# A graph network on one core: ranks by source placed in two halves of 392 columns, and rows normalised four blocks a turn

## The reference

```python
edge_index = jnp.stack([src, dst])
h = jnp.maximum(_layernorm(x, axis=-1), 0.0)
x = x + _L0_gnn_ref(h, src, dst, edge_weight, L0_gnn_weight, L0_gnn_b)
h = jnp.maximum(_layernorm(x, axis=-1), 0.0)
x = x + _L1_gnn_ref(h, edge_index, edge_attr_128, node_vec1, node_vec1_n2, ...)
h = jnp.maximum(_layernorm(x, axis=-1), 0.0)
x = x + _L2_gnn_ref(h, edge_index, edge_weight, ...)
h = jnp.maximum(_layernorm(x, axis=-1), 0.0)
x = x + _L3_gnn_ref(h, L3_gnn_relvectors, ..., src, dst, edge_type_16)
return x
```

## Time and profile before

| what | before |
|---|---|
| median of 3 timed runs | 5067.49 us (5064.09 to 5072.64) |
| span of the profiled execution | 6606.6 us |
| time of the profiled execution outside its span | not given |
| DVE, busy share of the span | 56% |
| POOL, busy share of the span | 54% |
| TensorE (PE), busy share of the span | 57% |
| preparation in the trace | 0 to 1492.6 us |
| scatters of records, L462 | 784, 808.2 us busy |

### The profile page before, as it was taken

How to read it: one execution, slowest core, us unless ns; L and a number is a source line. 1 busy time by engine, 2 the same in 40 slices (tenths; PEclk the granted TensorE clock), 3 DMA queues, 4 the chain that set the end, 5 groups by cost and what they waited for, 6 DMA issues and landing times. The chain is left out here.

```text
span 6606.6 us, 98591 instructions
## 1 busy us (share of the span) xinstructions
PE 3748.5 (57%) x15612; PEld 2748.4 (42%) x15613; DVE 3700.6 (56%) x12722; ACT 1475.8 (22%) x5078; POOL 3595.2 (54%) x4000
## 2 busy tenths in 40 slices
PE   0000020005776776776677777777779667777676
PEld 0000010004555554555455555555559534444443
DVE  5249691006666666666555555555557656555555
ACT  1000000000111111111455455555546301100000
POOL 4640686755655565555444444444437766655554
PEclk9999999998887888888788888878889878888888
DMA  4320224454444444444333333333332233333332
GB/s 119 85 68 0 73 83 89 118 148 120 127 127 123 125 128 124 127 128 111 93 94 94 96 95 95 94 93 94 97 95 86 89 88 94 91 91 90 90 90 72
DMA packets 505174, 651.54 MB, mean 99 GB/s; under 512 B 86113, under 2 KB 381294, under 8 KB 504944
## 3 DMA queue, kind: packets, MB, share of 16 engines
q0 software_dynamic: 150160, 395.04, 20.9%
q1 hardware_dynamic: 354913, 255.45, 14.3%
HBM read 550.09 MB, written 100.06 MB: 98 GB/s over the span
## 5 line engine op out<-in xcount | busy, mean ns | idle before, releaser
L1398 POOL DMA_INDIRECT a_row<-h_rows,a_idx x832 | 789.8, 949 | 944.0 <-PE a_p_s L1504 396.0
L2005 POOL DMA_INDIRECT r_row<-h_rows,r_idx x832 | 798.3, 960 | 528.7 <-PE r_p_s L2046 267.9
L462 POOL DMA_INDIRECT src_records<-rec,pos_slot x784 | 808.2, 1031 | 419.6 <-issue 250.3
L983 POOL DMA_INDIRECT s_row<-h_rows,s_rec x832 | 804.5, 967 | 281.0 <-issue 242.2
L1018 PE MATMUL s_sums<-s_row,s_hotw 128*128 128x256 f32 x1664 | 661.3, 484 | 519.5 <-DVE s_hotw L1203 315.3
L2046 PE MATMUL r_p_s<-r_row,r_hot 128*128 128x272 f32 x1664 | 644.8, 502 | 362.8 <-DVE r_row L2182 171.9
L1481 PE MATMUL a_p_q<-nodes,a_hotT 128*128 x1664 | 665.0, 486 | 314.9 <-DVE a_score L1551 188.9
L1211 DVE TENSOR_TENSOR nodes<-nodes,s_sums 128x385 f32 x832 | 455.5, 548 | 509.1 <-remote 290.8
L1504 PE MATMUL a_p_s<-a_row,a_masked 128*128 128x257 f32 x1664 | 588.7, 439 | 178.1 <-issue 124.3
L2046 PEld LDWEIGHTS r_p_s<-r_row,r_hot 128*128 128x128 f32 x1664 | 353.1, 234 | 678.8 <-issue 296.2
L1551 DVE CUSTOM_DVE_ANT_0 a_prod<-a_p_q,a_row 128x258 f32<-128x258 f32 x832 | 352.7, 424 | 415.9 <-DMA s_rec<-src_records 187.6
(11 more groups left out here) (315 smaller groups left out, 7511.6 us busy)
## 6 DMA issues: line engine op xcount, KB each, us to landing
s_rec<-src_records SPq DMA_DIRECT2D x832, 66.0 KB
a_locs<-dloc_rows SPq DMA_DIRECT2D x208, 256.0 KB
rec<-in_edge_attr SPq DMA_DIRECT2D x98, 448.0 KB
s_row<-h_rows,s_rec POOLq DMA_INDIRECT x832
a_row<-h_rows,a_idx POOLq DMA_INDIRECT x832
r_row<-h_rows,r_idx POOLq DMA_INDIRECT x832
src_records<-rec,pos_slot POOLq DMA_INDIRECT x784
x_rows<-X SPq DMA_DIRECT2D x1, 6272.0 KB
```

The source lines that it names most:

```text
L462: gp.indirect_dma_start(out=src_records, out_offset=bass.IndirectOffsetOnAxis(ap=pos_slot[:, k:k + 1], axis=0), in_=rec[:, k, :], in_offse ...
L983: gp.indirect_dma_start(out=row[:, k % R, :], out_offset=None, in_=env["h0_rows"], in_offset=bass.IndirectOffsetOnAxis(ap=rec[:, k % R, DS ...
L1398: gp.indirect_dma_start(out=row[:, k, 0:D], out_offset=None, in_=env["h2_rows"], in_offset=bass.IndirectOffsetOnAxis(ap=idx[:, k:k + 1], a ...
L2005: gp.indirect_dma_start(out=row[:, k % R, 0:D], out_offset=None, in_=env["h3_rows"], in_offset=bass.IndirectOffsetOnAxis(ap=idx[:, k:k + 1 ...
```

## The change

The ranks are placed in two halves of 392 columns, written out one after the other, in place of eight segments of 98 in a loop. The place writes to `pos["src"]` directly, and `pos_seg` with its two copies goes. The second half has no carry. The helper unrolls three blocks a turn (`RB`) in place of six. `ranked_steps` rises twice, by 392. POOL's power and its wait move from before turn 16 to before turn 22 (`ROOT_TURN`). ScalarE's wait for `rstd_ready` moves from before turn 16 to before turn 28 (`FIRST_FOUR`), and it normalises four blocks in each of the turns 28 to 39.

```diff
-    SEG = STEPS // 8
+    SEG = STEPS // 2
...
-    PAIRS = (BLOCKS - 1) // 2
-    FIRST_PAIR = 16
+    RB = 3
+    AT_ONCE = 4
+    FOURS = (BLOCKS - 1) // AT_ONCE
+    ROOT_TURN, FIRST_FOUR = 22, 28
...
-        eq = sb(ctx, "eq", [EP, SB, SEG], U16)
-        cum_seg = sb(ctx, "cum_seg", [EP, SB, SEG])
+        eq = sb(ctx, "eq", [EP, RB, SEG], U16)
+        cum_seg = sb(ctx, "cum_seg", [EP, RB, SEG])
...
-                scatters((0, FIRST_PAIR))
+                scatters((0, ROOT_TURN))
                 gp.wait_ge(stats_ready, 1)
                 nc.gpsimd.tensor_tensor(rstd[:], vare[:], half[:], ALU.pow).then_inc(rstd_ready, 1)
-                scatters((FIRST_PAIR, WIN_TURN))
+                scatters((ROOT_TURN, WIN_TURN))
...
-                with ac.Fori(0, FIRST_PAIR) as turn:
+                with ac.Fori(0, FIRST_FOUR) as turn:
                     complete(turn)
                 ac.wait_ge(rstd_ready, 2)
                 ac.wait_ge(loaded_x, 32)
-                with ac.Fori(0, PAIRS) as pair_i:
-                    complete(pair_i + FIRST_PAIR)
-                    normalise(pair_i * 2)
-                    normalise(pair_i * 2 + 1)
+                with ac.Fori(0, FOURS) as four:
+                    complete(four + FIRST_FOUR)
+                    for k in range(AT_ONCE):
+                        normalise(four * AT_ONCE + k)
...
+                def place_half(seg):
+                    cols = slice(seg * SEG, (seg + 1) * SEG)
+                    n = seg * BLOCKS
...
+                        nc.vector.copy_predicated(pos["src"][:, cols], eq[:, k, :], cum_seg[:, k, :]).then_inc(placed, 1)
...
+                    if seg == 0:
+                        in_turns(ve, BLOCKS, RB, (2, place), (2, carry), (1, count_up), (0, match))
+                        own_wait(ve, carried, n + BLOCKS)
+                    else:
+                        in_turns(ve, BLOCKS, RB, (2, place), (1, count_up), (0, match))
+                    own_wait(ve, placed, n + (BLOCKS + 1))
+                    ve.nop().then_inc(ranked_steps, SEG)
```

More of the change, by code:

```diff
@@ L250, in prepare @@
     HOT_TURNS = STEPS // 16
+    assert FOURS * AT_ONCE == BLOCKS - 1 and ROOT_TURN < FIRST_FOUR and FIRST_FOUR + FOURS < STORE_TURN
     assert HOT_TURNS * 16 == STEPS and SEGS * SEG == STEPS and WIN_TURN + (CHUNKS - 1) * WIN_APART < REC_TURNS
@@ L263, in prepare @@
         lo_d = sb(ctx, "lo_d", [EP, STEPS], BF16)
-        eq = sb(ctx, "eq", [EP, SB, SEG], U16)
-        cum_seg = sb(ctx, "cum_seg", [EP, SB, SEG])
+        eq = sb(ctx, "eq", [EP, RB, SEG], U16)
+        cum_seg = sb(ctx, "cum_seg", [EP, RB, SEG])
         eq_f = sb(ctx, "eq_f", [EP, 2, STEPS], BF16)
         cum = sb(ctx, "cum", [EP, STEPS])
-        pos_seg = sb(ctx, "pos_seg", [EP, SEG])
         edge = sb(ctx, "edge", [P, BLOCKS])
@@ L352, in prepare @@
         spare_set, spare_placed = sem("spare_set"), sem("spare_placed")
-        hi_ready, act_counted, seg_moved = sem("hi_ready"), sem("act_counted"), sem("seg_moved")
+        hi_ready, act_counted = sem("hi_ready"), sem("act_counted")
         dst_ranked, filled, drow_ready, drow_stored = (sem(n) for n in ("dst_ranked", "filled", "drow_ready", "drow_stored"))
@@ L562, in _ @@
                 ac.wait_ge(loaded_x, 32)
-                with ac.Fori(0, PAIRS) as pair_i:
-                    complete(pair_i + FIRST_PAIR)
-                    normalise(pair_i * 2)
-                    normalise(pair_i * 2 + 1)
+                with ac.Fori(0, FOURS) as four:
+                    complete(four + FIRST_FOUR)
+                    for k in range(AT_ONCE):
+                        normalise(four * AT_ONCE + k)
                 normalise(BLOCKS - 1)
-                with ac.Fori(FIRST_PAIR + PAIRS, REC_TURNS) as turn:
+                with ac.Fori(FIRST_FOUR + FOURS, REC_TURNS) as turn:
                     complete(turn)
@@ L651, in rank @@
                                                           in1=first[0:EP, :], op0=ALU.add, op1=ALU.add))
-                def place_segments():
-                    ve.nop().then_inc(placed, 1)
[L655 to L686, removed]
@@ new lines, in place_half, with match, count_up, place @@
+                def place_half(seg):
+                    cols = slice(seg * SEG, (seg + 1) * SEG)
+                    n = seg * BLOCKS
+                    def match(i, k, opening, g):
+                        nc.vector.tensor_scalar(eq[:, k, :], hi[:, cols], c["iota"][0:EP, bass.ds(i, 1)], None,
+                                                ALU.is_equal).then_inc(matched, 1)
+                    def count_up(i, k, opening, g):
+                        ve.wait_ge(matched, i + (n + 1))
+                        nc.vector.tensor_tensor_scan(cum_seg[:, k, :], ones_row[:], eq[:, k, :], base[:, bass.ds(i, 1)],
+                                                     ALU.mult, ALU.add).then_inc(scanned, 1)
+                    def place(i, k, opening, g):
+                        ve.wait_ge(scanned, i + (n + 1))
+                        own_wait(ve, placed, i + (n + 1))
+                        nc.vector.copy_predicated(pos["src"][:, cols], eq[:, k, :], cum_seg[:, k, :]).then_inc(placed, 1)
+                    def carry(i, k, opening, g):
+                        nc.vector.tensor_scalar(base[:, bass.ds(i, 1)], cum_seg[:, k, SEG - 1:SEG], 0.0, None,
+                                                ALU.add).then_inc(carried, 1)
+                    if seg == 0:
[5 more added lines that the diff above has]
+                    ve.nop().then_inc(ranked_steps, SEG)
@@ L688, in by_rank, with place_halves @@
+                def place_halves():
+                    ve.nop().then_inc(placed, 1)
+                    for seg in range(SEGS):
+                        place_half(seg)
                 def by_rank(order):
@@ L741, in _ @@
                 rank("src", hi)
-                place_segments()
+                place_halves()
                 ve.wait_ge(loaded_x, 32)
```

## The result

The changed kernel takes **5112.32 us** (median, 5110.26 to 5117.2) against 5069.8 (5064.09 to 5072.64, four runs now) for the kernel before, ratio 1.0088 [1.0074, 1.0102]. The forecast was 5114. Sign and size are right, but the sum hid two errors that cancel, which is luck, and the reading of the first profile was wrong.

The account below looks back on a forecast made before the run. The preparation was taken to be bound by a chain: ranks of the first columns, then 784 POOL scatters in a row. Terms +61 - 20 - 2 + 8 = +47 us on 5067.5 gave 5114 us, range 4980 to 5155.

Parts of the forecast that it names:

- 1 start of the scatters: In the preparation, POOL's first scatter must wait for 392 columns instead of 98: +61 us (+35 to +74).
- 2 DVE's total: Placing of ranks ends near 236 us instead of 372, but nobody uses the 136 us: 0.
- 3 wait for the statistics: POOL's wait for `vare` before the power goes, since the power moves to turn 22: -20 us (0 to 40).
- 4 ScalarE: The 1.88 us between POOL's power and the next scatter go, as ScalarE's result is needed only from turn 28: -2 us.
- 5 scatters beside long DVE work: Some 80 POOL scatters run slower beside DVE instructions of about 1 us: +8 us (-10 to +20).
- the 272 us: POOL's waits for DVE in the first trace's preparation, about 221 + 26 + 25 us, held to be the recording's.
- The argument from TensorE: TensorE's 3687.62 us after the preparation leave 1379.9 of 5067.5, so at least 113 us of the traced preparation must go.
- The frame without the recording: Unrecorded kernel before: ranks end at 372 us, POOL could take the power at 398 and comes there at 401.5.
- near 6400: Recorded span forecast for the changed kernel, by the same steps against the first recorded span, summing to -205 us.
- Equal: Scatter spacing near 1.0 us unrecorded, so the old kernel waited 50 to 73 us for statistics: about 5069 us; chance 0.16.
- Faster: POOL's scatters hold DVE back in timed runs too, and long blocks cure it: 4862 us in full; chance 0.26.
- Slower than forecast: Start at upper bound, no old wait, full port price: +92 us, 5159; top of the likeliest case (slower, 0.58).

Follow-up runs that it names:

- e1: The kernel before, unchanged, recorded a second time (the second trace): 5062.85 us, ratio 0.9997.
- e2: The kernel before with the power before turn 22, ScalarE's wait before turn 28 and four blocks a turn: 5062.19 us, ratio 0.9996.
- e9: The changed kernel with 16 more empty DVE instructions (FILLERS 168): 5115.96 us, ratio 1.0102 to the kernel before.
- e3: The changed kernel with power and ScalarE's wait back before turn 16, two blocks a turn: 5119.59 us, ratio 1.0109 to the kernel before.
- e6: The changed kernel with eight segments of 98 columns, RB 6, FILLERS 318: 5054.15 us, ratio 0.9976 to the kernel before.
- e8: The changed kernel with segments of 32, seven of 96 and 80 columns, RB 6, FILLERS 227: 5040.39 us, ratio 0.9954 to the kernel before.
- e10: The kernel before with 181 more empty DVE instructions at the end of the preparation (FILLERS 333): 5185.93 us, ratio 1.0237.

## Why the forecast held, and where it was wrong

| term | forecast | measured |
|---|---|---|
| 1 start of the scatters | +61 (35 to 74) | +42 |
| 2 DVE's total | 0 | 0 (`vare` 175 us earlier, nothing gained by it) |
| 3 wait for the statistics | -20 (0 to 40) | 0 |
| 4 ScalarE | -2 | -2 |
| 5 scatters beside long DVE work | +8 (-10 to +20) | +13 |
| sum | +47 | +53 between the traces, +42.5 between the medians |

*What bounds.* Right: the chain "first ranks, then 784 scatters in a row" holds in the traces of all thirteen kernels and carries every difference in the preparation.

*Are the 272 us there.* The answer (no) was right, the reason given was not shown. That recording slows the execution by 30% does not hold in any later trace: the recorded execution of after took 5117.2 us where the median is 5112.32, and e1's took 5063.8 where it is 5062.85. The first trace shows one overlong execution. With it falls the use made of the rule on trace records (NOTIFIC — the notification-queue block, in the Trainium skill): no later run shows an engine throttled by its records, and whether the first trace does stays open. The argument from TensorE was weaker than it looked, too: it took 3687.62 us as what a normal execution needs, where the traces since have 3289.0 and 3300.4 in all. With the 3228.0 us of the later stages in the second trace, the same sum leaves 5067.5 - 3228.0 = 1839.5 us for a preparation of 1492.6, so it excludes no wait at all. The argument reached the right side by luck. The one thing that would have settled it is a second trace of the same kernel; a span more than 1530 us above every timed run says that it is another execution, not how the normal one looks. Why it was slow, in the preparation and after it, stays open; it did not happen again.

*The frame without the recording* was good: ranks done by 372 and statistics at 398 were forecast, and in the second trace (timeline of DVE) the last ranks are copied at 372.55 and `vare` is written at 398.60; POOL was forecast there at 401.5 and came at 408.66.

*Item 1* had the right mechanism and a wrong size: +42 in place of +61. What was mis-sized is the price of a longer block. From one scan to the next, a block of 392 columns takes 1.70 us, not 2.085. The timeline of DVE after shows it:

```profile
35.03 1.02 DVE L665 TENSOR_TENSOR_SCAN cum_seg<-ones_row,base,eq 128x392 f32<-128x392 bf16 x1
35.97 0.30 DVE L660 TENSOR_SCALAR eq<-hi,iota 128x392 uint16<-128x392 bf16 x1
36.18 0.60 DVE L671 COPY_PREDICATED pos_src<-eq,cum_seg 128x392 f32<-128x392 uint16 x1
36.67 0.14 DVE L675 TENSOR_SCALAR base<-cum_seg 128x1 f32 x1
36.73 1.02 DVE L665 TENSOR_TENSOR_SCAN cum_seg<-ones_row,base,eq 128x392 f32<-128x392 bf16 x1
```

The scan is 1024 ns, 604 more than at 98 columns and not 830: 2.05 ns a column. The slope of 2.8 that I drew came from two scans with different operand types (the one of 49 columns reads float32, the one of 98 bf16). The Trainium skill's rule in DVE: opcode table, instruction layouts, handler registers and perf-mode slots, section 6 (half throughput) would have given an estimate of +0.61 us a block, and the measured 0.604 bears it out. The match costs 56 ns more, not 150; the place 322, as forecast (310). The +50 worked out from that rule still lay 8 above the measured 42, in part by the match, and the lower bound of +35 lay 7 below it, with a scan at half its measured price.

*Item 3* failed by its premise: the spacing of 1.19 us was to reconcile the later stages with a recording cost that does not exist. At the traced spacing of 1.27 the text itself gave 0, and 0 it was. The 20 us taken off here and the 19 us too many of item 1 cancel. That is luck.

*Item 4* is right in the trace of after: POOL idles 2.1 us less, and the 1.89 after the power are gone. In e2 they are gone too and the sum of POOL's idle time among the scatters is no smaller (285.6 against 284.2), so the -2 is not shown to be worth anything.

*Item 5* was +13: the 62 scatters beside the wide blocks take 0.285 us more each than with DVE idle (1.251 - 0.966), 18 us, as I took it (0.3), but less falls away. Before, 229 scatters ran beside the short blocks; by the windows of that trace they are busy for 224.31 us, 0.98 each where I took 1.014, so about 3 us go, not 10.

*The total.* +53 between the traces and +42.5 between the medians are the same loss: the recorded execution of after is the longest of its four, and the one of before lies 6 us under the median of the four it is held against. The repeats e9 and e3, held against 15 and 14 runs, are 52 and 55 us over the kernel before. That 5114 and 5112.32 agree to 2 us is again luck.

*The rivals.* "Equal" needed a spacing near 1.0 us; it is 1.27. "Faster" needed DVE held back in timed runs; e1 excludes it. "Slower than forecast" had the start at its upper bound, +74, and it was +42. That the span would be "near 6400" was the first trace's number carried on, and wrong: it is 5115.1.

## What to carry to other kernels

When one engine works through a stream that ends a stage, what its *first* item waits for adds to the time in full; a shorter first segment wins (98 to 32 columns brought the first scatter from 74.1 us in e6 to 67.6 in e8, and the first layer from 1193.2 to 1185.5) and a saving on an engine that is not that stream is worth nothing (DVE has `vare` 175 us earlier here, at 223.86 in place of 398.60). If a profile's span is far above every timed run, take it again before costing anything by its waits. After an edit that changes the length of an engine's code, look at the packets of the instruction queue and for "issue" gaps of equal length in later loops: here 75 empty instructions decided 126 us of one stage (1194 against 1068), more than any part of the change.

## What the hardware showed beyond that

- The place of a DVE loop in its code costs up to 131 us of a stage with no work changed (e10; 122 between the medians): some 4.9 us each time round, 295 instruction packets instead of 73. Yet 100 extra packets in after cost nothing (e9), so their number alone does not tell; the gaps in front of one instruction of the loop do.
- A scatter is lengthened by DVE instructions beside it, from 0.97 to at most 1.34 us beside blocks of 392 columns, barely (0.98 in the mean) beside those of 98. Which of a block's instructions does it, the scan or the predicated copy, no run here separates. DVE itself loses next to nothing: in the second trace of before a scan of 98 columns takes 419 ns ahead of the first scatter and 420 beside scatters, a match 227 and 244; in the changed kernel a scan of 392 takes 1025 and 1022.
- One recorded execution can be 30% long with the same code and data (span 6606.6 us against 5061.7), in a pattern (DVE gaps beside POOL's scatters) that reads like a mechanism.
